# Normalisation of a conv and attention hybrid on one core: sums of squares and spreading of the roots on parts of the TensorE array

## The reference, cut to what matters

```python
def _ln_t(v, eps=1e-05):
    m = jnp.mean(v, axis=-1, keepdims=True)
    s = jnp.var(v, axis=-1, keepdims=True)
    return (v - m) / jnp.sqrt(s + eps)

t = t + _L2_attn_ref(_ln_t(t), ...)
t = t + _L2_ffn_ref(_ln_t(t), ...)
t = t + _L3_attn_ref(_ln_t(t), ...)
t = t + _L3_ffn_ref(_ln_t(t), ...)
```

## Time and profile before

| | us |
|---|---|
| median of 3 runs | 4673.47 |
| lowest and highest | 4671.93, 4682.45 |
| the profiled execution | 4675.34 |
| its span | 4673.6 |
| TensorE busy, share of the span | 3941.6, 84% |
| VectorE | 2888.8, 62% |
| ScalarE | 2026.5, 43% |
| GpSimd | 910.0, 19% |

### The profile page before, as it was taken

The page is one execution under the profiler, slowest core; times in us unless marked ns, Lnnn a source line. Parts: engine busy times, 40 slices in busy tenths (PEclk is TensorE's granted clock), DMA queues, the critical chain, the costliest instruction groups (busy, mean ns, idle before and its releaser), DMA issues. The chain is left out here.

```text
span 4673.6 us, 171666 instructions
## 1 busy us (share of the span) xinstructions
PE 3941.6 (84%) x71052; PEld 2298.1 (49%) x71053; DVE 2888.8 (62%) x6291; ACT 2026.5 (43%) x4155; POOL 910.0 (19%) x2323
## 2 busy tenths in 40 slices
PE   3578999889799997788888679999999999885995
PEld 1226666434366664345555434544545445444763
DVE  3546777410377774477888638858858858843343
ACT  1113444221234441366666417757747747602221
POOL 0001111000011110255555301111111111105022
PEclk7789999889899997899999789999999999977997
DMA  1000000000000000100000000000000000025223
GB/s 48 0 9 1 0 0 0 4 18 0 8 1 0 0 0 4 43 1 1 1 1 1 1 11 1 0 1 0 0 1 0 0 1 0 1 88 189 65 90 102
DMA packets 47250, 80.84 MB, mean 17 GB/s; under 512 B 7120, under 2 KB 38128, under 8 KB 46064
## 3 DMA queue, kind: packets, MB, share of 16 engines
q1 hardware_dynamic: 40944, 61.84, 3.9%
q0 software_dynamic: 6144, 16.79, 1.1%
HBM read 45.05 MB, written 33.55 MB: 17 GB/s over the span
## 5 line engine op out<-in xcount | busy, mean ns | idle before, releaser
L1688 PE MATMUL psum<-hm_ex,hm_mix 128*128 128x512 f32 x1024 | 510.2, 621 | 42.3 <-ACT hm_Aq L1768 38.3
L1754 ACT ACTIVATE hm_ex<-psum,hm_nm 128x1024 f32<-128x1024 f32 x256 | 285.7, 1116 | 297.4 <-DVE hm_nm L1812 297.4
L1688 PEld LDWEIGHTS psum<-hm_ex,hm_mix 128*128 128x128 f32 x1024 | 175.5, 191 | 352.0 <-issue 344.3
L1827 DVE COPY hm_A<-psum 128x1024 f32<-128x1024 f32 x256 | 312.9, 1222 | 51.2 <-PE psum L1697 47.7
L1822 DVE TENSOR_SCALAR_CACHE_REDUCE hm_plus<-hm_Aq,hm_cbcol,hm_sums 128x1024 f32<-128x1024 f32 x256 | 340.4, 1330 | 0.0
L1812 DVE TENSOR_REDUCE hm_nm<-psum 128x1 f32<-128x1024 f32 x256 | 311.0, 1215 | 12.8 <-PE psum L1676 12.8
L1697 PEld LDWEIGHTS psum<-K,hm_Aq 128*128 128x128 f32 x2048 | 236.6, 140 | 149.9 <-issue 145.3
L678 PE MATMUL psum<-fw_w,fw_stage 128*128 (+1 forms) x512 | 245.1, 563 | 67.6 <-DVE fw_vh L852 50.8
L1759 ACT ACTIVATE hm_junk<-hm_Aq 128x1024 f32<-128x1024 f32 x256 | 270.6, 1057 | 30.3
L1676 PE MATMUL psum<-hm_kt,hm_qd 64*32 64x512 f32 x4096 | 279.6, 604 | 0.0
L1234 ACT ACTIVATE pt_signs<-pt_acts,pt_tb 128x1024 f32<-128x1024 f32 (+1 forms) x224 | 227.5, 1017 | 116.4 <-POOL pt_tb L1101 95.4
(11 more groups left out here) (364 smaller groups left out, 8103.1 us busy)
## 6 DMA issues: line engine op xcount, KB each, us to landing
ex_rows_in<-ex_zero SPq DMA_DIRECT2D x2, 5120.0 KB, 25.0
ex_xs<-ex_rows_in SPq DMA_DIRECT2D x80, 128.0 KB, 2.0
ex_rows_out<-ex_ys SPq DMA_DIRECT2D x80, 128.0 KB, 1.7
ex_w<-in_ex_w SPq DMA_DIRECT2D x2, 4096.0 KB, 23.1
X<-in_x SPq DMA_DIRECT2D x2, 2048.0 KB, 11.9
out_y<-X SPq DMA_DIRECT2D x2, 2048.0 KB, 9.0
ff_w<-in_ff_w SPq DMA_DIRECT2D x2, 1024.0 KB, 5.7
pt_w_proc<-in_pt_proc SPq DMA_DIRECT2D x1, 2048.0 KB, 7.6
```

What stands on the lines that cost most here:

```text
L1688: mm = pe.matmul(bank[4 + c], mix[:, u, :], ex[:, u, 512 * c:512 * c + 512], start=True, stop=True)
L1754: act.activation(ex[:, u, :], flat2(psum[:, 2 * u:2 * u + 2, :]), ACT.Exp, bias=nm[:, u:u + 1], accum_out=rsum[:, u:u + 1]).then_inc(s_ex, 1)
L1827: dve.tensor_copy(A[:, :, :, QT_ * t:QT_ * t + QT_], flat2(psum[:, 6:8, :]).rearrange("p (m g n) -> p m g n", m=MT, g=HEADS)).then_inc(s_a ...
```

## The change

The sums of squares of the four groups of a half now stand side by side: group r uses columns 32r to 32r + 31 of the array, with 32 equal columns of `ones` as weights, and its result fills partitions 32r to 32r + 31 of bank 3. All four are issued together, first all with channel half 0, then all with half 1. The root and the reciprocal are then taken of all 128 partitions, 32 equal rows for each group. The spreading of group r uses rows 32r to 32r + 31 of the array, one of which has weight one, and writes all 128 partitions of bank 4 + r; the four of a half are issued together. `sq` has a slot for each group, `std` is one buffer for both halves, `pick` and its memsets are gone. The order on VectorE and ScalarE is kept. `mean`, `centre`, `square`, `scale` and `move` are as before.

```diff
-        sq = k.sb(f"{name}_sq", [P, 3, CH, GROUP], ctx)
-        std = k.sb(f"{name}_std", [HALF, 2, GROUP], ctx)
-        rstd = k.sb(f"{name}_rstd", [HALF, 2, GROUP], ctx)
+        sq = k.sb(f"{name}_sq", [P, NG, CH, GROUP], ctx)
+        std = k.sb(f"{name}_std", [P, GROUP], ctx)
+        rstd = k.sb(f"{name}_rstd", [P, 2, GROUP], ctx)
...
-                def squares(g):
-                    pe.wait_ge(s_sq, g + 1)
-                    r = g % HALF
+                def squares(b):
+                    if b > 0:
+                        pe.wait_ge(s_std, b)
+                    pe.wait_ge(s_sq, HALF * b + HALF)
                     for h in range(CH):
-                        mm = pe.matmul(bank[3 + g // HALF][0:HALF, :], pick[:, HALF - 1 - r:2 * HALF - 1 - r],
-                                       sq[:, g % 3, h, :], start=(r == 0 and h == 0),
-                                       stop=(r == HALF - 1 and h == CH - 1))
+                        for r in range(HALF):
+                            mm = pe.matmul(bank[3][rows(r), :], k.const("ones")[:, 0:32], sq[:, HALF * b + r, h, :],
+                                           start=(h == 0), stop=(h == CH - 1))
                     mm.then_inc(s_msq, 1)
 
-                def spread(g):
-                    pe.wait_ge(s_rstd, g // HALF + 1)
-                    if g >= 3:
-                        pe.wait_ge(s_out, g - 2)
-                    r = g % HALF
-                    pe.matmul(bank[5 + g % 3], k.const("ident")[0:HALF, r:r + 1].broadcast_to([HALF, P]),
-                              rstd[:, g // HALF, :], start=True, stop=True).then_inc(s_bc, 1)
-
-                mean(0)
-                mean(1)
-                pe.wait_ge(s_eps, 1)
-                for g in range(HALF):
-                    mean(g + 2)
-                    squares(g)
+                def spread(b):
+                    pe.wait_ge(s_rstd, b + 1)
+                    if b > 0:
+                        pe.wait_ge(s_out, HALF * b)
+                    for r in range(HALF):
+                        pe.matmul(bank[4 + r], k.const("ident")[rows(r), 32 * r:32 * r + 1].broadcast_to([32, P]),
+                                  rstd[rows(r), b, :], start=True, stop=True).then_inc(s_bc, 1)
+
+                for g in range(HALF + 2):
+                    mean(g)
+                squares(0)
                 mean(6)
                 mean(7)
-                for g in range(HALF):
-                    squares(HALF + g)
-                    spread(g)
-                for g in range(HALF):
-                    spread(HALF + g)
+                spread(0)
+                squares(1)
+                spread(1)
...
                 def root(b):
-                    act.wait_ge(s_msq, HALF * b + HALF)
-                    act.activation(std[:, b, :], bank[3 + b][0:HALF, :], ACT.Sqrt,
-                                   bias=eps[0:HALF, :]).then_inc(s_std, 1)
+                    act.wait_ge(s_msq, b + 1)
+                    if b > 0:
+                        act.wait_ge(s_rstd, b)
+                    act.activation(std[:, :], bank[3], ACT.Sqrt, bias=eps[:, :]).then_inc(s_std, 1)
...
-                    dve.reciprocal(rstd[:, b, :], std[:, b, :]).then_inc(s_rstd, 1)
+                    dve.reciprocal(rstd[:, b, :], std[:, :]).then_inc(s_rstd, 1)
```

More of the change, by code:

```diff
@@ L343, in norm_stage @@
     with ExitStack() as ctx:
-        sq = k.sb(f"{name}_sq", [P, 3, CH, GROUP], ctx)
-        std = k.sb(f"{name}_std", [HALF, 2, GROUP], ctx)
-        rstd = k.sb(f"{name}_rstd", [HALF, 2, GROUP], ctx)
+        sq = k.sb(f"{name}_sq", [P, NG, CH, GROUP], ctx)
+        std = k.sb(f"{name}_std", [P, GROUP], ctx)
+        rstd = k.sb(f"{name}_rstd", [P, 2, GROUP], ctx)
         eps = k.sb(f"{name}_eps", [P, 1], ctx)
-        pick = k.sb(f"{name}_pick", [P, 2 * HALF - 1], ctx)
-        s_zero, s_eps, s_mean, s_cen, s_sq, s_msq, s_std, s_rstd, s_bc, s_out, s_shift = (
-            k.sem(f"s_{name}_{n}") for n in "zero eps mean cen sq msq std rstd bc out shift".split())
+        s_eps, s_mean, s_cen, s_sq, s_msq, s_std, s_rstd, s_bc, s_out, s_shift = (
+            k.sem(f"s_{name}_{n}") for n in "eps mean cen sq msq std rstd bc out shift".split())
         bank = k.bank
@@ L353, in norm_stage @@
         both = lambda ap: ap.unsqueeze(1).broadcast_to([P, CH, GROUP])
+        rows = lambda r: slice(32 * r, 32 * r + 32)
         with nc.Block() as block:
@@ L356, in _ @@
             def _(pool):
[L357 to L360, removed]
+                pool.memset(eps[:, :], EPS).then_inc(s_eps, 1)
             @block.tensor
@@ L409, in square @@
                     act.wait_ge(s_cen, g + 1)
-                    if g >= 3:
-                        act.wait_ge(s_msq, g - 2)
-                    act.activation(sq[:, g % 3, :, :], at(dst, g), ACT.Square).then_inc(s_sq, 1)
+                    act.activation(sq[:, g, :, :], at(dst, g), ACT.Square).then_inc(s_sq, 1)
                 def root(b):
-                    act.wait_ge(s_msq, HALF * b + HALF)
-                    act.activation(std[:, b, :], bank[3 + b][0:HALF, :], ACT.Sqrt,
-                                   bias=eps[0:HALF, :]).then_inc(s_std, 1)
+                    act.wait_ge(s_msq, b + 1)
+                    if b > 0:
+                        act.wait_ge(s_rstd, b)
+                    act.activation(std[:, :], bank[3], ACT.Sqrt, bias=eps[:, :]).then_inc(s_std, 1)
                 def move(g):
@@ L450, in scale @@
                     if gain is None:
-                        dve.tensor_tensor(at(dst, g), at(dst, g), both(bank[5 + g % 3]), ALU.mult).then_inc(s_out, 1)
+                        dve.tensor_tensor(at(dst, g), at(dst, g), both(bank[4 + g % HALF]), ALU.mult).then_inc(s_out, 1)
                     else:
@@ L454, in scale @@
                             to = at(dst, g)[:, h, :]
-                            last = dve.scalar_tensor_tensor(to, to, k.vec(gain, h), bank[5 + g % 3], ALU.mult, ALU.mult)
+                            last = dve.scalar_tensor_tensor(to, to, k.vec(gain, h), bank[4 + g % HALF], ALU.mult, ALU.mult)
                         last.then_inc(s_out, 1)
```

## The result

| | before | changed | ratio |
|---|---|---|---|
| median, us | 4674.55 | 4594.82 | 0.9828 (95% interval 0.9814 to 0.9843) |
| lowest to highest | 4671.93 to 4682.45 | 4592.56 to 4597.95 | |
| span of the profiled execution | 4673.6 | 4596.1 | |

What follows compares the result with a forecast made beforehand. TensorE was taken to set the pace in the seven barrier-bounded normalisation stages; 4 x 12.96 + 3 x 11.81 = 87.3 us saved gave 4586.2 from the median and 4588.0 from the profiled execution, stated as 4587 us, range 4576 to 4602.

Steps and rivals of the forecast that it cites:

- The overlap of column parts: A half's squares on four 32-column parts: 1.71 us plus 0.17 for spacing, 1.88 in all, against 6.83 one by one.
- the drain at a change of tiling mode: TensorE, mean and squares: two changes of form cost 0.31 us, already in the trace; before has more such changes.
- The stage ln5: Worked example of a stage without gain: 12.96 us saved, the end at 4160.81 instead of 4173.77.
- three points: In ln5, from the first matmul: reciprocal(0) after 13.24 us, reciprocal(1) after 23.36, end of last scaling after 33.50.
- reciprocal and root: Covering 128 partitions in place of 4 was taken at no cost: reciprocal 3.3 us, activation 689 ns against 678.
- (d): Clock: squares(1) at 1.2 GHz, 5 us in all, 4592; or spread(1) kept at 2.4 GHz, 4580; no separate chance.
- Rival (a): Second half's spreadings: row parts don't overlap, scalings 1.71 us apart, 10 us in all, 4597; chance 9%.
- Rival (b): Squares: column parts don't overlap, squares(0) costs 4.95 us more, only 25 us saved in all, 4649; chance 4%.
- (c): Squares: parts one after another, array emptied between records, 32 us slower, near 4706; decides from 8.7 us per squares; chance 2%.
- The sum: Savings over seven stages: 4 x 12.96 without gain plus 3 x 11.81 with gain and shift, 87.3 us.

Runs made afterwards that it cites:

- all serial: Changed kernel's order, waits and banks, but squares and spreadings one after another, nothing side by side: 4656.33 us, ratio to the kernel before 0.9960.
- columns alone: Changed kernel with squares still side by side, but each spreading on all 128 rows, one after another: 4593.95 us, ratio to the kernel before 0.9827.
- rows alone: Changed kernel with spreadings still side by side, but a half's squares as 8 matmuls one after another: 4656.56 us, ratio to the kernel before 0.9964.

## Why the prediction was right, and where it was off

**The overlap of column parts** was taken from lines 1707 and 1649, as 1.71 us of records plus 0.17. It is 1.92 us for the burst, tail included, and squares(0) to root is 2.00 (4073.55 to 4075.55 in ln5) for 2.09 forecast. The 0.17 was too much: the row of 1.09 us leaves 0.07 when two records and the tail are taken off, and the burst is 0.04 longer than the four records of 1.88. This overlap is 62 to 66 us of the 80 to 84, as the two halves of the change run apart show; the order alone gives 19. The Trainium skill, "TensorE: Matmul & The Clock Gate", Measured speedup vs the span model, has 2.38 for three column parts and 3.07 for four row parts. Here four column parts gave 7.03 / 1.92 = 3.7 and four row parts 3.70 / 1.14 = 3.2, more for each part than either figure. Of the drain at a change of tiling mode that the Trainium skill, "TensorEngine Tiling (Array Packing)", Key Properties, names, no run here shows more than the 0.1 to 0.2 us that before already had.

**The stage ln5** went as worked out, each of three points within 0.2 us; reciprocal and root cost on 128 partitions what they cost on 4 (3.35 for 3.34, 0.69 for 0.68).

**The clock** is the step that was mis-sized. It stood under (d) as a possible 5 us, and the sum was made without it. It fell before the second half's squares in four stages and among them in two; against the 10.00 and 10.74 that d is with a high clock, this cost 0.9 to 1.2 us in ln2, ln3 and ln4, 0.2 in lnff and lnf1 and nothing in lnf0 and ln5, 3.6 in all. The sum had let TensorE's idle time ahead of the squares cost nothing, since nothing waits for an idle engine; but the next work on it goes slower. lnf1 lost another 1.7 us to the clock at its start: its 24 records of six means took 12.23 us, those of lnf0 10.54.

```profile
267.81 10.54 PE L365 MATMUL psum<-Y,K 128*128 128x512 f32 x24 [1.82 <-PEq L98]
...
1168.67 12.23 PE L365 MATMUL psum<-Y,K 128*128 128x512 f32 x24 [2.00 <-PEq L98]
```

Before, this stage kept the high clock (first centring 1.99 us behind the first matmul, now 3.06). The pause of 2.00 us ahead of it is in both kernels, and in the changed one the granted clock is still 1.00 through it and falls some 0.8 us behind the first matmul (0.91 in the microsecond from 1168.6, 0.50 in the next). It did so again in the second trace of the changed kernel (38.84 us for the stage). The twelve traces fall apart by one thing: where the last four spreadings go one after another (before, all serial, columns alone) lnf1 starts at the high clock, in the nine others at the low one. What would tie them to a stage that starts 230 us behind those of lnff, no run here settles.

**Rival (a)**, row parts that don't overlap, is refuted as a fact (1.14 us for eight records), and its price of 10 us was wrong as well: with the spreadings one after another the kernel loses nothing. **Rival (b)** is refuted, and its price was near: 4649 forecast for serial squares with the rest as changed, 4656.6 measured; serial squares at the low clock, as in the row of 8.80 us above, are one part of the 8 us between. **(c)**, the slower one, needed 8.7 us per squares; in parts they took 1.92, and 3.64 at the low clock. (Even one after another they took 7.03 at the high clock; rows alone had up to 10.11, in lnff, where the clock was low for a part of them.)

**The sum** was 87.3; the stages gave 84.1 in the trace. The clock took 3.6 and 1.7 of it; with these put back each stage gained 0.2 to 0.6 us more than forecast, 2.1 in all, which partly hid the loss. By the medians it is 79.7 in one comparison and 84.3 in the other, with some 6 us that lie outside the stages in the one trace.

## What to carry to other kernels

Here a matmul that filled few columns or rows of the array cost as much as a full one (1.88 us for the four records of four columns, 1.98 for those of 128); four of them on parts of their own cost little more than one, if they are ready together, and this order has to be made for them. Shorten what stands on the path and ask of the rest what it did besides its work: here slow matmuls that nobody waited for kept TensorE's clock up, and two idle ones did that as well. Once TensorE no longer sets the pace, count elements per partition on the engine that does: the reciprocal of 128 partitions took no longer than that of 4 (3.35 and 3.34 us), and with 128 elements in each instead of 512 it took 0.95.

## What the runs showed of the hardware that I had not expected

- The clock can fall within a short wait. In ln3 it fell between 1821 and 1822, under 2 us behind the last matmul, after TensorE had been busy 1.14 us with a wait on either side; in ln5 the same pattern left it at 2.4 GHz (1.00 from 4078.8 to 4087.8). In ln2 before it fell over 3 us behind the last matmul, which ended at 233.57 (it is 0.96 in the half microsecond before 237.00 and 0.50 in the next).
- Records that queue on separate parts overlap in depth: 16 records, four to a part, end 1.92 us behind their start, and 64 of 128 columns take 1.95.
- On row parts with 128 columns of weights short records are dear: 32 records of 128 moving columns take 2.81 us, eight of 512 take 1.14, the same number of columns in all. The 32 weight loads stand without a gap for 2.62 of the 2.81 us in ln5, which points at them; no run takes the two apart.
